# Softplus attention in groups of two stages, and the causal mask added in PSUM by VectorE

## The chip, the cores and the metric

The kernel runs on one core of one Trainium2 chip. The metric is device time in microseconds (us) of one execution. Before the change three runs took 6087.67 us in the median, 6085.19 to 6090.55.

TensorE (PE in the profile) multiplies matrices from SBUF into PSUM, VectorE (DVE), ScalarE (ACT) and GpSimd (POOL) work on elements, and SyncE (SP) issues DMAs. The engines run side by side and wait for each other through semaphores.

## What is computed

Eight layers follow each other on `x` of 8 x 256 x 128 in float32. The change touches two of them, one early and one late:

```python
def _L0_attn_b_ref(X, Wq, bq, Wk, bk, Wv, bv, sink_scalars, v_nulls, Wo, bo):   # softplus attention
    scores = jnp.einsum('bhtd,bhsd->bhts', q, k) * ATTN_SCALE     # 64 heads of 8
    w = jax.nn.softplus(scores / denom)
    w = jnp.where(causal[None, None], w, 0.0)
    w = w * jax.nn.sigmoid(SCALE * w)
    alpha = 1.0 / (jnp.sum(w, axis=-1, keepdims=True) + sinks + 1e-06)
    ...
def _L1_attn_b_ref(x, wq, wk, wv, wo):                            # causal softmax attention
    scores = jnp.einsum('bhqd,bhkd->bhqk', q, k) * scale          # 16 heads of 8
    scores = jnp.where(causal_mask, -jnp.inf, scores)
    local_max = jnp.max(scores, axis=-1, keepdims=True)
    exp_scores = jnp.exp(scores - local_max)
    local_sum = jnp.sum(exp_scores, axis=-1, keepdims=True)
    attn_num = jnp.einsum('bhqk,bhkd->bhqd', exp_scores, v)
    attn_out = attn_num / (local_sum + 1e-08)
```

## The kernel before

The program is eight parts, one after the other; at the end of each all engines meet. Order, tiles and semaphore counts are written out by hand for each engine, so the order in the source is the order on each engine. The parts before, between and behind the two touched ones are the same code before and after.

**Softplus attention (`b0_...`).** One batch entry has 16 units (a unit is one key head with its four query branches), that is 8 pairs and 4 stages of two pairs. Each pair has 3 chunks (keys of block 0 against queries of block 0, then 1 against 1, then 0 against 1), so a stage has 6 chunks and the batch entry 24; eight entries give 32 stages and 192 chunks. A chunk is 128 x 1024 elements and goes this way:

- `scores` (PE, L2220): two float32 matmuls with 32-row keys into two PSUM banks. Chunk kind k always uses banks 2k and 2k+1, so chunk i waits until VectorE is done with chunk i-3 (`b0_soft`).
- `soft` (ACT, L2302 and L2304): exp from PSUM to the buffer `b0_w`, then ln(1+x) in place. Both are in one table set, which `log_exp_tables` (its load is recorded at L312) brings in.
- `larger` (DVE, L2375): the larger of that and the score.
- `weigh` (ACT, L2310): one Silu over all of a pair, 3072 columns; it needs another table set, so a load stands ahead of it.
- `mask` (POOL, L2461): zeroes the upper triangle, one instruction for each unit, two for each pair.
- `heads` (PE, L2234 and L2237): weights times values into PSUM bank 6, then `evacuate` (DVE, L2380), `turn` (PE, four transposes, L2245, bank 7) and `context` (DVE, L2394 to L2408).

`b0_w` holds 8 units, four pairs. So the first chunk of pair p waits in `soft` until `heads` of pair p-4 is done (`b0_out`, L2300). ACT does `soft` of a stage, then `weigh` of that stage. On PE the scores of the next stage stand between the heads of this one (`stage`, L2248 to L2260), and the first three scores of the stage after that stand at its end. Before the first of each six scores PE waits for masked keys (`masked_keys`, DVE L2368), which DVE makes at the end of its stage.

**Causal attention (`b1_...`).** 8 batch entries of 8 units, 64 units; a unit is two heads. Per unit: PE puts the mask into two PSUM banks with an identity matmul (L1922, 256 columns for each of two heads) and adds the scores over it (L1928, three pieces of 128 columns for each head); DVE takes two maxima (`shift`, L2064 and L2065); ACT does four exps with row sums (`exps`, L2020); DVE inverts the sums (`reciprocals`, L2071 and L2073); POOL scales the probabilities (L2097); PE transposes them (`turn`, L1938, six); ACT copies the result to SBUF (`copy_turned`, L2028); PE multiplies with the values (`heads`, L1954). PE runs `scores(u+2)`, `turn(u-1)`, `heads(u-2)` in that order, and `scores(u+2)` waits until `exps(u)` has read the same two banks. Once for each entry PE also projects keys and queries (L1903) and values (L1911) and DVE makes four masked copies of the queries (`mask`, L2059).

A float32 matmul in the source is two instructions in the trace, a transpose is one.

## Time and profile before

| | us |
|---|---|
| median of three runs | 6087.67 |
| profiled execution | 6097.43 |
| its span in the trace | 6095.6 |
| softplus attention, first exp to last Silu, 2747 to 3446 | 699 |
| causal attention, first mask matmul to last heads, 5643 to 5887 | 244 |

| engine | busy us | share of the span |
|---|---|---|
| PE (matmul) | 4834.0 | 79% |
| PE weight load | 3081.1 | 51% |
| ACT | 4289.3 | 70% |
| DVE | 4177.5 | 69% |
| POOL | 2641.0 | 43% |

The shares are averages over parts with different limits, so the two touched parts have to be read by themselves. PEclk in the profile is the TensorE clock that the chip granted, as a share of 2.4 GHz; it is either 1.00 or 0.50 (1.2 GHz), and a figure between is a stretch with both. Over the whole run it is 0.873.

### The profile page before, as it was taken

The page shows a single profiled execution, that of the slowest core. Times are in us where ns is not written, and L with a number is a line of the kernel's source. Part 1 is how long each engine was busy: PE and PEld are TensorE (multiplying, and loading weights), DVE is VectorE, ACT ScalarE, POOL GpSimd, SP SyncE. Part 2 cuts the span into 40 slices and gives each one's busy share as a digit, 9 for nine tenths or more (in the row PEclk, how much of TensorE's full clock was granted, in tenths as well). Part 3 has the DMA queues.
Part 4 walks back from the last instruction along what each step waited for, and adds up shares of the span by engine and source line. Part 5 has one row for each costly group of instructions (what it writes and reads, how often), then busy time and mean ns, then how long its engine had stood idle before and what let it go on. Part 6 is the DMA issues. An engine that isn't in the chain of part 4 may idle for free. (4 is left out here: it accounts for less than half of the span.)

```text
span 6095.6 us, 174670 instructions
## 1 busy us (share of the span) xinstructions
PE 4834.0 (79%) x68176; PEld 3081.1 (51%) x68176; DVE 4177.5 (69%) x6507; ACT 4289.3 (70%) x8575; POOL 2641.0 (43%) x1155
## 2 busy tenths in 40 slices
PE   1000089999999999987777799999999999969998
PEld 0000056666666666642333366666666666624754
DVE  6777767777777777765555477777777777656446
ACT  4444267777777777738999777777777777648668
POOL 0000066555555656513444466565656565400430
PEclk6555589999999999986666699999999999979999
DMA  1000022222222222210000122222222222100000
GB/s 51 0 0 0 29 52 65 61 65 58 62 65 61 65 62 65 54 27 1 0 0 0 31 51 65 62 65 62 64 62 65 62 65 61 48 10 4 1 3 8
DMA packets 181346, 248.41 MB, mean 41 GB/s; under 512 B 52077, under 2 KB 80233, under 8 KB 180073
## 3 DMA queue, kind: packets, MB, share of 16 engines
q1 hardware_dynamic: 176264, 221.95, 14.7%
q10 hardware_dynamic: 4320, 15.73, 0.9%
q8 instruction: 548, 8.98, 0.6%
q14 instruction: 214, 1.75, 0.1%
HBM read 43.50 MB, written 5.24 MB: 8 GB/s over the span
## 5 line engine op out<-in xcount | busy, mean ns | idle before, releaser
L402 PE MATMUL PS<-arena 128*128 128x512 f32 x2304 | 1202.9, 619 | 29.2 <-ACT arena L766 17.7
L1089 POOL TENSOR_TENSOR lns<-arena 128x1024 f32<-128x1024 f32 x192 | 543.8, 2832 | 1009.7 <-DVE arena L975 749.9
L1089 POOL TENSOR_TENSOR arena<-arena 128x1024 f32<-128x1024 f32 x192 | 548.4, 2856 | 468.7 <-DVE arena L975 468.7
L964 DVE TENSOR_REDUCE arena<-arena 128x32 f32<-128x2048 f32 x192 | 438.9, 2286 | 431.3 <-ACT arena L766 431.3
L461 PEld LDWEIGHTS PS<-arena 64*64 64x64 f32 x24576 | 492.9, 136 | 202.2 <-issue 201.4
L1486 PE MATMUL PS<-arena 128*128 128x512 f32 x8 | 5.9, 900 | 700.3 <-DVE arena L1415 700.3
L1092 POOL TENSOR_TENSOR lnc<-arena 128x1024 f32<-128x1024 f32 x192 | 548.5, 2857 | 0.0
L1092 POOL TENSOR_TENSOR arena<-arena 128x1024 f32<-128x1024 f32 x192 | 547.7, 2853 | 0.0
L461 PE MATMUL PS<-arena 64*64 64x32 f32 x24576 | 523.2, 223 | 11.2 <-issue 10.0
L402 PEld LDWEIGHTS PS<-arena 128*128 128x128 f32 x2304 | 378.0, 192 | 253.4 <-issue 113.9
L2461 POOL TENSOR_TENSOR arena<-arena 128x1024 f32<-128x1024 f32 x128 | 298.0, 2357 | 478.3 <-ACT arena L2310 478.3
L765 ACT ACTIVATE arena<-PS 128x512 f32<-128x512 f32 x768 | 471.8, 614 | 32.4 <-PE PS L402 20.9
L766 ACT ACTIVATE arena<-PS 128x512 f32<-128x512 f32 x768 | 476.6, 621 | 0.0
L768 ACT ACTIVATE arena<-PS 128x512 f32<-128x512 f32 x384 | 230.3, 600 | 339.1 <-PE PS L402 338.5
L975 DVE TENSOR_TENSOR arena<-arena 128x1024 f32<-128x1024 f32 x384 | 458.8, 1236 | 8.9 <-ACT arena L781 8.9
L790 ACT ACTIVATE arena<-PS 128x512 f32<-128x512 f32 x768 | 446.4, 620 | 13.7 <-PE PS L419 6.8
L2220 PE MATMUL PS<-arena 32*128 32x512 f32 x768 | 324.7, 968 | 162.7 <-DVE arena L2368 132.7
L959 DVE TENSOR_TENSOR arena<-arena 128x1024 f32<-128x1024 f32 x192 | 429.8, 2239 | 25.5 <-PE PS L422 5.3
L477 PE MATMUL PS<-arena 128*128 128x256 f32 x1536 | 360.1, 386 | 65.6 <-ACT arena L815 65.6
L434 PE MATMUL PS<-arena 64*32 64x64 f32 x24576 | 381.5, 217 | 32.8 <-issue 25.1
L2375 DVE SCALAR_TENSOR_TENSOR arena<-arena,PS 128x1024 f32<-128x1024 f32 x192 | 230.7, 1215 | 242.0 <-ACT arena L2304 241.7
L434 PEld LDWEIGHTS PS<-arena 64*32 64x32 f32 x24576 | 341.8, 105 | 84.6 <-issue 84.4
(278 smaller groups left out, 10919.4 us busy)
## 6 DMA issues: line engine op xcount, KB each, us to landing
arena<-arena SPq DMA_DIRECT2D x2880, 64.0 KB, 2.0
arena<-in_L_ffn_Wqkv ACTq DMA_DIRECT2D x30, 512.0 KB, 4.2
arena<-in_L_ffn_Wo SPq DMA_DIRECT2D x48, 128.0 KB
scratch<-arena SPq DMA_DIRECT2D x4, 1024.0 KB, 4.7
arena<-scratch SPq DMA_DIRECT2D x4, 1024.0 KB, 7.7
arena<-in_L_ffn_W SPq DMA_DIRECT2D x12, 341.0 KB, 2.9
arena<-in_L_ffn_Wqkv SPq DMA_DIRECT2D x6, 512.0 KB, 5.0
arena<-in_ffn_scales SPq DMA_DIRECT2D x12, 128.0 KB, 3.0
```

The lines of the kernel that those rows point to most:

```text
L402: pe.matmul(PS[:, QKV + bank, :], xs[uu % 2][:, par * P:(par + 1) * P], w, start=True, stop=True).then_inc(qkv_ready, 1)
L434: last = pe.matmul(PS[w * WIN:(w + 1) * WIN, SCORE + s, m * FD:(m + 1) * FD], qT[s * FD:(s + 1) * FD, m, w * WIN:(w + 1) * WIN], KT[uu % 2 ...
L461: last = pe.matmul(PS[(m % 2) * FD:(m % 2 + 1) * FD, HEAD + head_index(tt, s) % 2, at:at + WIN], VW[par][rows, w, m * FD:(m + 1) * FD], PT ...
L477: last = pe.matmul(PS[:, HEAD + n % 2, 0:T], Wo[:, m, :], AT[uu][:, m, :], start=(m == 0), stop=(m == PAIRS - 1))
L765: act.activation(chunk(raws[tt % 2], c), PS[:, QKV + bank, :], ACT.Copy)
L766: act.activation(chunk(sq, c), PS[:, QKV + bank, :], ACT.Square).then_inc(qkv_copied, 1)
L790: act.activation(to, PS[:, TURN + n % 2, :].rearrange("p (m t) -> p m t", m=4), ACT.Copy)\
L959: dve.tensor_tensor(EN.rearrange("p (m s e) -> p s m e", s=2, e=FD), E.rearrange("p (s m e) -> p s m e", s=2, e=FD), rc, ALU.mult).then_in ...
L964: dve.tensor_reduce(nrm[:, 3, :], h3(sq), AX_X, ALU.add).then_inc(norm2_own, 1)
L975: dve.tensor_tensor(h3(raw[:, part]), h3(raw[:, part]), rn, ALU.mult).then_inc(u_ready, 1)
L1089: pool.tensor_tensor(halves(heads(t2)), halves(heads(raws[par]))[:, :, ::-1, :], sine, ALU.mult)\
L1092: pool.tensor_tensor(heads(t1), heads(raws[par]), cosine, ALU.mult).then_inc(t1_ready, 1)
```

## The change

**Softplus attention.** Stages are taken two by two. ACT runs `soft` of two stages, 12 chunks, and then `weigh` of both, four Silus; `log_exp_tables` is called before every second `soft` only. `stage` on PE and DVE becomes `group`, of four pairs and 12 chunks, with a new interleaving: 15 scores instead of 9 stand ahead of the loop, and in a group PE runs heads, score 3, turn, heads, scores 4 and 5, turn, heads, scores 6 and 7, turn, score 8, heads, score 9, turn, scores 10 to 14 (numbers count from the next group's first chunk). DVE makes the masked keys of the stages ahead in `keys_ahead`, once behind `larger` 6 and once behind `larger` 11. The buffers are the same.

**Causal attention.** The mask matmul goes. The scores start their banks themselves, in two pieces for each head (128 and 256 columns) where there were three. DVE adds the mask in place in PSUM, 128 x 512 elements over the two banks, waits for its own add, and then takes the two maxima.

```diff
@@ causal attention, PE
-                for s in range(2):
-                    pe.matmul(PS[:, (u % 2) * 2 + s, 0:2 * P], ident[:], b1_mask, start=True, stop=False,
-                              skip_group_check=True)
-                for q, lo, hi in ((0, 0, P), (P, P, 2 * P), (P, 2 * P, BLOCKS)):
+                for q, lo, hi in ((0, 0, P), (P, P, BLOCKS)):
                     for s in range(2):
...
-                                         b1_ks[b % 2][rows, lo:hi], start=(lo == 2 * P), stop=True, skip_group_check=True)
+                                         b1_ks[b % 2][rows, lo:hi], start=True, stop=True)
@@ causal attention, DVE
                 dve.wait_ge(hd_scores, first + u + 1)
+                diagonal = PS[:, (u % 2) * 2:(u % 2) * 2 + 2, 0:2 * P]
+                mask = b1_mask.rearrange("p (o j) -> p o j", o=1).broadcast_to([P, 2, 2 * P])
+                dve.tensor_tensor(diagonal, diagonal, mask, ALU.add).then_inc(b1_added, 1)
+                dve.wait_ge(b1_added, u + 1)
                 dve.tensor_reduce(st[:, 0:2], PS[:, (u % 2) * 2:(u % 2) * 2 + 2, 0:P], AX_X, ALU.max, negate=True)
@@ softplus attention, ACT
             def soft(b, n):
-                log_exp_tables(act)
+                if n % 2 == 0:
+                    log_exp_tables(act)
...
-                for n in range(STAGES):
-                    soft(b, n)
-                    weigh(b, n)
+                for n in range(GROUPS_B0):
+                    soft(b, 2 * n)
+                    soft(b, 2 * n + 1)
+                    weigh(b, 2 * n)
+                    weigh(b, 2 * n + 1)
@@ softplus attention, DVE, in group()
+                evacuate(b, 4 * n + 2)
+                ahead(6)
+                if not final:
+                    keys_ahead(b, 2 * n + 4, 12 * (n + 1) + 5)
+                context(b, 4 * n + 2)
...
+                ahead(9, 10, 11)
+                if not final:
+                    keys_ahead(b, 2 * n + 5, 12 * (n + 1) + 11)
```

The order on PE in softplus attention, from the written-out last two entries. Before, a stage goes on so from the second half of its first pair's heads (L2234 and L2237 are heads, four such rows for each pair, L2220 a score, x2 for each chunk, L2245 a turn):

```order
L2234 MATMUL PS<-arena 32x256 x4
L2237 MATMUL PS<-arena 32x128 x4
L2220 MATMUL PS<-arena 128x512 x2
L2245 MATMUL PS<-ident,arena 128x128 x4
L2220 MATMUL PS<-arena 128x512 x2
L2234 MATMUL PS<-arena 32x256 x4
L2237 MATMUL PS<-arena 32x128 x4
```

With the change a group goes on so from the last heads row of its first pair (L2237 and L2240 are heads, L2223 a score, L2248 a turn):

```order
L2240 MATMUL PS<-arena 32x128 x4
L2223 MATMUL PS<-arena 128x512 x2
L2248 MATMUL PS<-ident,arena 128x128 x4
L2237 MATMUL PS<-arena 32x256 x4
L2240 MATMUL PS<-arena 32x128 x4
L2237 MATMUL PS<-arena 32x256 x4
L2240 MATMUL PS<-arena 32x128 x4
L2223 MATMUL PS<-arena 128x512 x4
L2248 MATMUL PS<-ident,arena 128x128 x4
```

The second pair's heads moved ahead of the second score, and still stand behind the first one.

On ACT, between the last ln of a stage and the first exp of the next, it was before:

```order
L2304 ACTIVATE arena<-arena 128x2x512
L2310 ACT_TABLE_LOAD
L2310 ACTIVATE arena<-arena 128x3072
L2309 REGISTER_ALU
L2310 ACTIVATE arena<-arena 128x3072
L312 ACT_TABLE_LOAD
```

and after 12 chunks it is now (L2314 is the ln, L2320 the Silu):

```order
L2314 ACTIVATE arena<-arena 128x2x512
L2320 ACT_TABLE_LOAD
L2320 ACTIVATE arena<-arena 128x3072 x3
L2319 REGISTER_ALU
L2320 ACTIVATE arena<-arena 128x3072
L312 ACT_TABLE_LOAD
```

The two loads now enclose four Silus in place of two.

On PE in causal attention one unit was before:

```order
L1922 MATMUL PS<-arena,ident 128x256 x2
L1928 MATMUL PS<-arena 128x128 x6
L1938 MATMUL PS<-ident,arena 128x128 x6
L1954 MATMUL PS<-arena 32x256 x2
L1954 MATMUL PS<-arena 32x128 x2
```

and is now (L1926 are the scores, L1936 the transposes, L1952 the heads):

```order
L1926 MATMUL PS<-arena 128x128 x2
L1926 MATMUL PS<-arena 128x256 x2
L1936 MATMUL PS<-ident,arena 128x128 x6
L1952 MATMUL PS<-arena 32x256 x2
L1952 MATMUL PS<-arena 32x128 x2
```

The identity matmuls with full rows and columns are gone, and the score pieces of 128 columns became one of 256.

## Rows read from the trace of the kernel before

**Rows 1.** Busy us by stretch: PE, weight load, DVE, ACT, POOL; PEclk; DMA share, GB/s.
```profile
2747.00:3446.00 699.00, 526.82 (x3001) 216.47 (x3003) 364.01 (x798) 640.50 (x511) 291.26 (x126) 0.62 0.00 1
...
5470.00:5590.00 120.00, 120.00 (x908) 64.00 (x908) 82.66 (x163) 109.48 (x454) 13.97 (x24) 1.00 0.01 1
...
5650.00:5660.00 10.00, 10.00 (x45) 7.49 (x44) 3.82 (x12) 4.36 (x18) 4.22 (x6) 0.50 0.01 2
5661.00:5876.00 215.00, 215.00 (x1823) 151.36 (x1821) 90.53 (x264) 151.54 (x569) 94.24 (x117) 1.00 0.01 1
```
**Rows 2.** Groups by line, 2640 to 3480: shapes xcount | busy us, mean ns | idle before.
```profile
L2304 ACT ACTIVATE arena<-arena 128x1024 f32<-128x1024 f32 x192 | 202.9, 1057 | 6.1
L2302 ACT ACTIVATE arena<-PS 128x1024 f32<-128x1024 f32 x192 | 194.6, 1013 | 51.1 <-PE PS L2220 50.7
...
L2310 ACT ACT_TABLE_LOAD x32 | 41.1, 1283 | 0.6
```
**Rows 3.** Timeline of ACT: start us, us, engine line op [idle before <-releaser].
```profile
3005.26 1.28 ACT L2310 ACT_TABLE_LOAD   x1
3006.55 5.42 ACT L2310 ACTIVATE arena<-arena 128x3072 f32<-128x3072 f32 x2
3011.99 1.28 ACT L312 ACT_TABLE_LOAD   x1
...
3026.23 1.28 ACT L2310 ACT_TABLE_LOAD   x1
...
3049.32 1.28 ACT L2310 ACT_TABLE_LOAD   x1
```
**Rows 4.** Timeline of PE, DVE and POOL in softplus attention.
```profile
3009.46 9.32 POOL L2461 TENSOR_TENSOR arena<-arena 128x1024 f32<-128x1024 f32 x4 [11.60 <-ACT arena L2310]
...
3015.43 1.22 DVE L2375 SCALAR_TENSOR_TENSOR arena<-arena,PS 128x1024 f32<-128x1024 f32 x1 [7.65 <-ACT arena L2304]
...
3022.92 1.13 PE L2220 MATMUL PS<-arena 32*128 32x512 f32 x4
...
3037.76 2.08 PE L2220 MATMUL PS<-arena 32*128 32x512 f32 x4 [0.33 <-DVE arena L2375]
...
3039.77 1.11 PE L2245 MATMUL PS<-ident,arena 128*128 128x128 f32 x4
...
3042.82 1.08 PE L2234 MATMUL PS<-arena 128*32 128x256 f32 x8
...
3044.95 0.66 PE L2237 MATMUL PS<-arena 128*32 128x128 f32 x8
```
**Rows 5.** Timeline of the end of softplus attention: last Silus, last context.
```profile
3440.59 5.42 ACT L2310 ACTIVATE arena<-arena 128x3072 f32<-128x3072 f32 x2
...
3457.35 0.42 DVE L2408 TENSOR_REDUCE XN<-arena 128x16 f32<-128x64 f32 x2
```
**Rows 6.** Timeline of PE over one unit of causal attention, at PEclk 1.00.
```profile
5740.95 1.13 PE L1922 MATMUL PS<-arena,ident 128*128 128x256 f32 x4
...
5742.02 0.94 PE L1928 MATMUL PS<-arena 32*128 32x128 f32 x12
...
5742.88 0.88 PE L1938 MATMUL PS<-ident,arena 128*128 128x128 f32 x6
...
5743.69 0.84 PE L1954 MATMUL PS<-arena 128*32 128x256 f32 x8
```
**Rows 7.** Timeline of PE early in causal attention, where PEclk rises from 0.50.
```profile
5655.92 1.65 PE L1928 MATMUL PS<-arena 32*128 32x128 f32 x12
5657.50 1.54 PE L1938 MATMUL PS<-ident,arena 128*128 128x128 f32 x6
5658.84 1.91 PE L1903 MATMUL PS<-XN,arena 128*128 128x256 f32 x4
5660.54 1.33 PE L1922 MATMUL PS<-arena,ident 128*128 128x256 f32 x4
```
**Rows 8.** Timeline: the nearest DVE operation with an operand in PSUM and 512 columns.
```profile
5889.69 0.69 DVE L2085 TENSOR_TENSOR XO<-XO,PS 128x512 f32<-128x512 f32 x1 [0.17 <-PE PS L1980]
```

More of the change, by code:

```diff
@@ L2103, in program @@
         STAGES = UNITS // 4
+        GROUPS_B0 = STAGES // 2
         BLOCK_KEYS = ((0, 0), (1, 1), (0, 1))
@@ L2246, in turn, with group, ahead @@
                 last.then_inc(b0_turned, 1)
-            def stage(b, par, n, final):
-                def ahead(c):
-                    if not (final and (6 * (n + 1) + c) >= CHUNKS):
-                        scores(b, par, 6 * (n + 1) + c)
-                heads(b, par, 2 * n)
-                ahead(3)
-                turn(b, 2 * n)
-                ahead(4)
-                heads(b, par, 2 * n + 1)
-                ahead(5)
-                turn(b, 2 * n + 1)
-                for c in range(6, 9):
-                    ahead(c)
-            for i in range(9):
+            def group(b, par, n, final):
+                def ahead(*chunks):
+                    for c in chunks:
+                        if not (final and (12 * (n + 1) + c) >= CHUNKS):
+                            scores(b, par, 12 * (n + 1) + c)
+                heads(b, par, 4 * n)
+                ahead(3)
+                turn(b, 4 * n)
+                heads(b, par, 4 * n + 1)
+                ahead(4, 5)
+                turn(b, 4 * n + 1)
+                heads(b, par, 4 * n + 2)
+                ahead(6, 7)
+                turn(b, 4 * n + 2)
+                ahead(8)
+                heads(b, par, 4 * n + 3)
+                ahead(9)
+                turn(b, 4 * n + 3)
+                ahead(10, 11, 12, 13, 14)
+            for i in range(15):
                 scores(0, 0, i)
@@ L2265, in b0_tensor @@
                 for par in range(2):
-                    for n in range(STAGES):
-                        stage(it * 2 + par, par, n, False)
+                    for n in range(GROUPS_B0):
+                        group(it * 2 + par, par, n, False)
             for par in range(2):
-                for n in range(STAGES):
-                    stage(B - 2 + par, par, n, par == 1)
+                for n in range(GROUPS_B0):
+                    group(B - 2 + par, par, n, par == 1)
             pe.wait_ge(b0_done, PAIRS_B0 * B + 1)
@@ L2312, in b0_scalar @@
             with act.Fori(0, B) as b:
-                for n in range(STAGES):
-                    soft(b, n)
-                    weigh(b, n)
+                for n in range(GROUPS_B0):
+                    soft(b, 2 * n)
+                    soft(b, 2 * n + 1)
+                    weigh(b, 2 * n)
+                    weigh(b, 2 * n + 1)
             for c in range(NCH):
@@ L2434, in b0_vector @@
             masked_keys(0, 1)
-            for i in range(6):
+            for i in range(12):
                 larger(0, i)
+                if i == 6:
+                    keys_ahead(0, 2, 5)
+            keys_ahead(0, 3, 11)
             with dve.Fori(0, B // 2 - 1) as it:
                 for par in range(2):
-                    for n in range(STAGES):
-                        stage(it * 2 + par, par, n, False)
+                    for n in range(GROUPS_B0):
+                        group(it * 2 + par, par, n, False)
             for par in range(2):
-                for n in range(STAGES):
-                    stage(B - 2 + par, par, n, None if par == 0 else True)
+                for n in range(GROUPS_B0):
+                    group(B - 2 + par, par, n, None if par == 0 else True)
             for c in range(NCH):
```

27 lines of the change are left out of this document (16 added, 11 removed).

## The prediction

> **What bounds the kernel now.** I read the busy times by stretch first, then the groups by line and the waits, then the timeline of one stage or unit, because the shares of the whole run mix parts with different limits. The two touched parts have different bounds.
>
> In softplus attention ACT is the bound: busy 640.5 of 699 us [rows 1]. Its stage is two table loads, two Silus and six exp and ln. From the first load of the timeline to the end of the second there are 8.01 us (1.28 + 5.42 + 1.28 and small steps), and an exp and an ln take 1.013 + 1.057 us, 2.0 from exp to exp since neighbours overlap [rows 2, 3]. So ACT's own stage is 8.0 + 12.0 = 20.0 us, and 32 of them 641. The other 58 us are nearly all one wait, exp for the scores, 51.1 us [rows 2]. PE is no bound by its work, but its clock is: 0.62 on average [rows 1]. A score takes 2.01 us at half clock and 1.13 at full [rows 4]. Stages are therefore uneven, 20.97 and then 23.09 us between the same loads [rows 3].
>
> In causal attention PE is the bound without a gap: 215.00 of 215 us busy at a clock of 1.00, while ACT has 151.5, DVE 90.5 and POOL 94.2 [rows 1]. There are 59 units in that stretch, 3.64 us each. One unit is 1.07 us of mask matmul, 0.86 of scores, 0.81 of transposes and 0.77 of heads, start to start, 3.51 in all, and 0.13 for the projections [rows 6].
>
> **The change part by part.** The sum is made on the profiled execution, 6097.43 us; the median is 9.8 us lower, and I move only the difference over to it.
>
> *Table loads.* 16 groups need 32 loads where 32 stages needed 64. That is 32 x 1.283 = 41.1 us of ACT, on the path that sets the end [rows 3]. ACT's own group is 2.57 + 4 x 2.71 + 24.1 = 37.5 us, against 40.1 for two stages. The trace shows no other cost of a switch: the Silus start at 3006.55, 1.29 us after the first load, and end at 3011.97, and the next load starts at 3011.99 [rows 3]. The Trainium skill (ScalarE: Activation LUTs, What ACT_TABLE_LOAD costs) gives 1283 ns for the load and about 1380 ns more for a drain with every switch. By it the saving would be 85 us; the load agrees with the trace, the drain is not to be seen beside it, and the sum goes by the row.
>
> *What the wide group gives back.* All eight units of `b0_w` now belong to one group, so the next group's exp for pair p waits for this group's heads of pair p, and on PE those heads stand behind scores which wait for ACT. I walk one group at half clock, with zero at its first Silu. ACT finishes four Silus and a load at 12.2 and the first exp and ln at 14.2. DVE takes 1.22 [rows 4], so score 3 starts at 15.5. POOL's masks are no limit: eight at 2.33 us from 2.9 on [rows 4], the second pair's ready at 12.2. From 15.5 on PE never waits: scores 3 to 11 (9 x 2.01), four turns (4 x 1.05) and three heads (3 x 2.7, from 3042.82 to 3045.61 less the overlap) are 30.4 us [rows 4], so score 11 is there at 45.9. An exp, an ln and a load later the next Silu starts: 49.2 us. Where two scores follow directly each takes about 0.2 less, which gives 48.2. The first wait is the new one: heads of the second pair end at 15.5 + 2.0 + 1.05 + 2.7 = 21.2, and ACT wants that buffer at 18.2. At full clock I estimate a turn at 0.6 and heads at 1.4; the same chain is 15.5 + 10.2 + 2.4 + 4.2 = 32.3, ACT's own work ends later, and only about 1.1 us of waits stay: 38.7.
>
> So a group costs 38.7 to 49.2 us, against 40.1 to 46.2 before, where the mean was 699 / 16 = 43.7, some 6 parts in 10 of the way up. The same place in the new range is about 44.0 to 44.3, and I take 44.0: 16 x 44.0 = 704, **+5 us**. The loads' 41 us are then all given back. At the end 11.8 us passed from the last Silu's end (3446.0) to the last context [rows 5]. Now eight masks (18.6) run from 2.9 us behind the first of four Silus, and heads, copy, turn and context (5 us) come after, 26.5 in all, 15.6 behind the last Silu: **+4 us**. Moved key copies (0.35 us of DVE) lie beside ACT's work, DVE being busy 364 of 699 us [rows 1]; uncovered all 32 would be 11 us. Softplus attention: **+9 us**, bounds -76 (16 x 38.7, with the end) and +92 (16 x 49.2).
>
> *The mask.* PE loses 1.07 us in each of 64 units [rows 6]. The wider score pieces stream the same columns, so I leave the scores at 0.86. DVE gains an add with a PSUM operand, 0.69 us by the nearest row [rows 8]; that row writes to SBUF, and writing back to PSUM could cost more, so 0.6 to 1.0 with the wait on itself, 0.74 taken. DVE's unit goes from 90.5 / 59 = 1.53 to 2.27, below the rest. Behind the add on DVE stand the reciprocals of the unit before, and POOL and then the transposes wait for those; POOL needs 94.2 / 59 = 1.6 us a unit and has room.
>
> **At full clock** PE is then at 3.64 - 1.07 = 2.57 us a unit and ACT at 151.5 / 59 = 2.57 [rows 1]. With two engines equal, four engines in a ring (scores, add and maxima, exps, then scores into the same banks), and four query masks on DVE in one unit of eight, I add 0.2 of waits: 2.77, or (3.64 - 2.77) x 64 = **-56 us**, 2.6 to 2.85 as bounds.
>
> **At half clock** scores are 1.5 us (12 pieces took 1.58), transposes 1.34, a projection 1.70 [rows 7], heads an estimated 1.4 from 0.77 at full [rows 6], the value projection an estimated 0.85. A unit is 4.25 + (1.70 + 0.85) / 8 = 4.6 us, PE again without a gap, 64 are 295 us. Before they took 244, the half-clock start included: **+51 us**.
>
> Which of the two holds decides the sign. Before, PE started this part at half clock and stayed there for a stretch busy 10.00 of 10 us [rows 1], so being busy was not enough. It rose to 1.00 at 5660.5, right behind transposes and a projection of full rows and columns with no gap [rows 7]. The mask matmul was the full-size half of PE's work in the start-up and a third in the steady unit; what is left beside the transposes is 32-row scores and 32-column heads. In softplus attention, where PE has just such scores and heads, the clock kept falling back and gave 0.62 [rows 1]. Against this stands the attention behind: only narrow matmuls, 1.00 for 120 us [rows 1]; but there PE has no gap, while here it would idle some 7%. I hold the fall the likelier, since the new part also has to climb from half clock first, with one projection in eight units to help.
>
> The sum: 6087.7 + 9 + 51 = **6148 us**.
>
> **The rivals.**
> 1. *The clock climbs and holds in causal attention*, decided at the first projection (second batch entry) and kept if PE's idle 0.2 us a unit does not matter. Speaks for it: the 120 us at 1.00 of the part behind. 6087.7 + 9 - 56 = 6041 us, faster.
> 2. *It switches back and forth*: half of the units at each level give 6087.7 + 9 - 2 = 6095, between 6060 and 6120.
> 3. *Softplus attention finds more full clock*, since PE has a long dense stretch in each group: half of the way from 44.0 to 38.7 is -42 us, 6106 with the forecast's causal part. It speaks against it that PE now idles from about 9 to 15.5 in each group, just before its dense stretch.
> 4. *A switch costs more than its load*, a drain that the rows hide under the last ln. By the page's rule named above 44 us more would go: 6104 us. Ends and starts 0.02 us apart [rows 3] leave it little room.
>
> **How the numbers follow.** Forecast 0.52, rival 1 0.28, rival 2 0.13, rival 3 0.05, rival 4 0.02. Faster by over 0.2% means under 6075.5, slower over 6099.9, about what a measurement can tell from no change. Rival 1 is all faster, of rival 2 0.04 faster, 0.05 same and 0.04 slower, of rivals 3 and 4 0.01 same: faster 0.32, same 0.06, slower 0.62. The forecast's own range is 6120 to 6175. The range takes in rival 1 with a unit of up to 2.6 us, 6030, and above the forecast a group of 45: 6164.
>
> **What would show it.** 32 loads for Silu become 16. A wait of exp for heads (L2300's semaphore) at the fourth chunk of a group of about 3 us where PEclk is 0.50. Groups of 44 us. In causal attention PEclk near 0.50, PE still without idle time, scores of 1.5 us, 4.6 us a unit; if PEclk is 1.00 there and units take 2.8 us, rival 1 is right and the step on the clock wrong. An add of over 1.0 us would make DVE the bound.

## The result and the profile after

The changed kernel takes **6017.5 us** (median of 3, 6001.08 to 6021.87) where the kernel before takes 6087.67. The ratio on record is 0.9876, 95% interval 0.9859 to 0.9893; the two medians themselves divide to 0.9885. It is 70 us faster; the prediction said 60 us slower. Its profiled execution has a span of 6015.7 us, 79.9 less than before.

Its page, the busy times and the granted clock in 40 slices:

```profile
span 6015.7 us, 173669 instructions
...
PE 4693.8 (78%) x67664; PEld 2987.3 (50%) x67664; DVE 4249.3 (71%) x6571; ACT 4238.6 (70%) x8543; POOL 2640.4 (44%) x1155
...
PEclk6555599999999999986666699999999999989999
```

PE is 140 us less busy than before, which is more than was gained, and DVE 72 us more. Where the time went is told by the starts of a few instructions in both traces. Five stretches: to the first exp of softplus attention; from there to its last Silu; on to its last context's reduction; the feed-forward part behind it, to its last matmul; and the causal part, from its first score or mask matmul to its last heads. Each is from start to start.

| us | to first exp | to last Silu | to last context | feed-forward | causal part |
|---|---|---|---|---|---|
| before | 2752.2 | 691.1 | 14.2 | 1874.8 | 243.7 |
| after | 2750.8 | 675.4 | 17.8 | 1866.2 | 185.7 |

**Causal attention gained 58.0 us and softplus attention 12.1**: together the 70 us of the medians. The other 9.8 us of the profiled executions are in code that the change does not touch. That code varies from one profiled execution to the next: over all kernels of this study the first stretch takes from 2735.8 to 2754.8 us, and the feed-forward part from 1866.2 to 1874.8 in the twelve kernels without extra matmuls in softplus attention. In the four that have such matmuls it takes 1876.4 to 1893.5, which is hardly chance and comes up again below. So the experiments are read by the two touched stretches first, and then by the whole time.

The changed kernel by stretch: us, busy (x instructions) of PE, PEld, DVE, ACT and POOL, granted clock, DMA share, GB/s. The first is softplus attention up to its last Silu, the third the start of the causal part, the fourth the rest of it to the last heads.

```profile
2750.80:3428.90 678.10, 460.29 (x2960) 183.11 (x2957) 386.38 (x775) 597.06 (x479) 286.10 (x124) 0.66 0.00 0
3428.90:3452.30 23.40, 18.51 (x134) 10.26 (x133) 12.87 (x43) 2.48 (x6) 10.91 (x6) 0.67 0.00 1
5617.00:5632.50 15.50, 10.87 (x50) 7.24 (x50) 10.93 (x24) 7.09 (x31) 3.39 (x5) 0.50 0.00 1
5632.50:5807.00 174.50, 163.65 (x1424) 103.38 (x1422) 132.83 (x330) 154.53 (x593) 100.25 (x124) 1.00 0.01 2
```

Against [rows 1]: softplus attention has a clock of 0.66 where it had 0.62, and the causal part is at 1.00 for all of its steady stretch, with PE idle for 10.9 of 174.5 us. By this row the prediction's own sign says that its step on the clock was wrong: it expected a clock near 0.50 there.

The groups of softplus attention (busy us, mean ns | idle before), to be held against [rows 2]:

```profile
L2314 ACT ACTIVATE arena<-arena 128x1024 f32<-128x1024 f32 x192 | 203.0, 1057 | 6.1
...
L2312 ACT ACTIVATE arena<-PS 128x1024 f32<-128x1024 f32 x192 | 194.3, 1012 | 79.5 <-PE PS L2240 49.6 <-PE PS L2223 28.9
...
L2320 ACT ACT_TABLE_LOAD x16 | 20.5, 1283 | 0.3
```

Of the 32 loads for Silu 16 are gone, and each exp and ln costs what it did. ACT's wait for PE grew from 51.1 to 79.5 us, and 49.6 of that is a wait for the heads (L2240 is their last matmul), where before 50.7 of the 51.1 us were for scores. One group on ACT's timeline shows it:

```profile
2774.94 1.28 ACT L2320 ACT_TABLE_LOAD   x1
2776.24 10.72 ACT L2320 ACTIVATE arena<-arena 128x3072 f32<-128x3072 f32 x4
2786.98 1.28 ACT L312 ACT_TABLE_LOAD   x1
...
2797.70 1.02 ACT L2312 ACTIVATE arena<-PS 128x1024 f32<-128x1024 f32 x1 [3.31 <-PE PS L2240]
...
2807.10 1.03 ACT L2312 ACTIVATE arena<-PS 128x1024 f32<-128x1024 f32 x1 [3.16 <-PE PS L2223]
...
2815.74 1.02 ACT L2312 ACTIVATE arena<-PS 128x1024 f32<-128x1024 f32 x1 [0.52 <-PE PS L2223]
...
2819.87 1.28 ACT L2320 ACT_TABLE_LOAD   x1
```

Four Silus, one load, three exp and ln, then 3.31 us of waiting at the fourth chunk; once more at the seventh, for a score. The 15 intervals from load to load are 44.9 us once and then 41.7 to 43.5. The same group, from its first Silu, up to where the clock rises and on to the next load:

```profile
2776.24:2806.30 30.06, 19.62 (x124) 8.01 (x124) 12.63 (x25) 24.15 (x17) 18.54 (x8) 0.50 0.00 1
2806.30:2819.90 13.60, 10.02 (x72) 4.08 (x68) 10.28 (x26) 12.07 (x13) 0.00 (x0) 1.00 0.00 1
```

In each interval the clock is at 1.00 for 13.6 to 17.1 us, late in PE's dense stretch.

The causal part by operation at full clock, the new add (L2064) and the three lines that it stands between:

```profile
L2018 ACT ACTIVATE arena<-PS,arena 128x128 f32<-128x128 f32 x122 | 48.4, 396 | 11.8 <-DVE arena L2067 11.8
L2064 DVE TENSOR_TENSOR PS<-PS,arena 128x512 f32<-128x512 f32 x60 | 41.7, 695 | 31.0 <-PE PS L1926 31.0
...
L1926 PEld LDWEIGHTS PS<-arena 32*128 32x128 f32 x480 | 31.4, 185 | 22.0 <-ACT arena L2018 9.8 <-issue 7.2 <-DVE arena L2057 4.1
L1926 PE MATMUL PS<-arena 32*128 32x128 f32 x240 | 29.4, 321 | 8.6 <-ACT arena L2018 6.4 <-DVE arena L2057 2.3
```

DVE waits for the scores, the exps for DVE's maxima (L2067), the scores for the exps and for the query masks (L2057). PE's 8.6 us are no wait of every unit: they are one of 0.91 us and one of 0.32 in each of seven batch entries, around the unit in which DVE makes the query masks (L2057). Apart from the end of the part PE has no other gap, so it is still the bound.

### The profile page after: what moved, and what is told of

Same layout as the page of the kernel before. It is cut to its first block and busy times, and to the rows that moved or that the text cites. A ratio compares the mean times of both kernels' runs of the same rounds, so it can differ in the third digit from the quotient of the medians.

```text
span 6015.7 us, 173669 instructions
## 1 busy us (share of the span) xinstructions
PE 4693.8 (78%) x67664; PEld 2987.3 (50%) x67664; DVE 4249.3 (71%) x6571; ACT 4238.6 (70%) x8543; POOL 2640.4 (44%) x1155
## 5 line engine op out<-in xcount | busy, mean ns | idle before, releaser
L461 PE MATMUL PS<-arena 64*64 64x32 f32 x24576 | 524.0, 223 | 10.5 <-issue 9.6
L765 ACT ACTIVATE arena<-PS 128x512 f32<-128x512 f32 x768 | 473.1, 616 | 29.7 <-PE PS L402 18.3
L2223 PE MATMUL PS<-arena 32*128 32x512 f32 x768 | 279.9, 835 | 129.0 <-DVE arena L2387 122.3
```

The costliest lines, as they stand in the source:

```text
L461: last = pe.matmul(PS[(m % 2) * FD:(m % 2 + 1) * FD, HEAD + head_index(tt, s) % 2, at:at + WIN], VW[par][rows, w, m * FD:(m + 1) * FD], PT ...
L765: act.activation(chunk(raws[tt % 2], c), PS[:, QKV + bank, :], ACT.Copy)
```

## The experiments

Stretches as in the table above; "softplus" is from the first exp to the last Silu. A clock is the mean of the whole stretch beside it, and a share of full clock s in the expectations is a mean of (1 + s) / 2. The ratio is to the kernel before on the same chip, where its median was between 6087.5 and 6095.86; medians of different kernels can be from different chips.

| kernel | median us | ratio, 95% interval | softplus us, clock | to last context | causal us, clock |
|---|---|---|---|---|---|
| before | 6087.67 | | 691.1, 0.62 | 14.2 | 243.7, 0.96 |
| after | 6017.5 | 0.9876, 0.9859 to 0.9893 | 675.4, 0.66 | 17.8 | 185.7, 0.97 |
| e1_group | 6077.95 | 0.9981, 0.9969 to 0.9993 | 673.6 | 18.3 | 243.7 |
| e2_mask | 6034.7 | 0.9907, 0.9890 to 0.9924 | 691.0 | 14.2 | 185.7 |
| e3_switch | 6069.16 | 0.9963, 0.9948 to 0.9977 | 726.6, 0.66 | 14.5 | 185.7 |
| e6_nomask | 6004.57 | 0.9858, 0.9841 to 0.9874 | 671.9 | 18.3 | 175.2, 0.97 |
| e5_add2 | 6042.61 | 0.9921, 0.9904 to 0.9937 | 672.0 | 18.3 | 217.8, 0.88 |
| e9_add4 | 6123.46 | 1.0054, 1.0037 to 1.0070 | 673.9 | 17.8 | 290.3, 0.79 |
| e16_gap | 6087.11 | 0.9992, 0.9980 to 1.0004 | 673.5 | 18.4 | 255.6, 0.84 |
| e4_order | 6045.55 | 0.9931, 0.9914 to 0.9949 | 704.4, 0.61 | 17.7 | 185.6 |
| e11_fill | 6037.11 | 0.9907, 0.9889 to 0.9923 | 676.3, 0.77 | 19.6 | 185.6 |
| e17_fill32 | 6032.72 | 0.9905, 0.9886 to 0.9923 | 679.4, 0.68 | 22.4 | 185.7 |
| e12_order_warm | 5993.16 | 0.9842, 0.9820 to 0.9865 | 648.4, 0.65 | 17.2 | 185.3 |
| e13_pace_narrow | 6024.29 | 0.9896, 0.9876 to 0.9916 | 659.0, 0.73 | 21.0 | 185.7 |
| e14_prefill_spread | 6009.86 | 0.9872, 0.9840 to 0.9904 | 651.6 | 17.2 | 176.5 |
| e15_both | 5985.57 | 0.9822, 0.9804 to 0.9839 | 648.3, 0.65 | 17.2 | 176.5, 0.97 |

### One half of the change at a time

e1_group is the kernel before with the part of the change in softplus attention alone, e2_mask with the part in causal attention alone (`b1_added`, the two score pieces, the add in `shift`).

> The kernel before with the softplus grouping alone (16 groups, 16 loads for Silu); the causal part keeps its mask matmul. My theory from the two traces: the part from the first exp to the last context went from 705.6 to 693.5 us, so this kernel is 10 to 16 us faster than before, about 6075. The prediction's step said +9, 6097. If most of the 70 us gained came from here by some effect on later parts, it would be below 6050.

> The kernel before with the causal mask on VectorE alone; softplus attention in stages as before. My theory from the two traces: the causal part took 243.7 us from its first mask matmul to its last heads and 185.7 in the changed kernel, and the clock rises to 1.00 within its first 20 us and holds, so -58 us, about 6030. The prediction's step said half clock and +51, 6139. If the clock of the causal part hung on what the softplus grouping left behind, this one would stay at 0.50 for longer and lie above 6060.

The halves add up: 0.9981 x 0.9907 = 0.9888 beside 0.9876 for both. Each stretch of a half is that of the changed kernel within 2 us, so neither half leans on the other, and both steps of the prediction had the wrong sign: +9 where it is about -12, and +51 where it is -58.

### What a table switch costs

```diff
                 for n in range(GROUPS_B0):
                     soft(b, 2 * n)
                     soft(b, 2 * n + 1)
                     weigh(b, 2 * n)
+                    log_exp_tables(act)
                     weigh(b, 2 * n + 1)
```

> The changed kernel with both function tables loaded once more in each group: exp and ln's table between the second and the third Silu, and Silu's again for the third, so 32 more loads and 16 more pairs of switches, at a point where everything behind waits for ACT. If a switch costs its load of 1.283 us and nothing else: +41 us, 6058 where the changed kernel has 6017. If each switch also drains for 1.4 us, as the prediction's rival 4 had it: +85, 6102. If PE's chain were the only bound of a group and the Silus not on it: under +20.

ACT's timeline in e3_switch:

```profile
3089.52 1.28 ACT L2320 ACT_TABLE_LOAD   x1
3090.81 5.42 ACT L2320 ACTIVATE arena<-arena 128x3072 f32<-128x3072 f32 x2
3096.25 1.28 ACT L312 ACT_TABLE_LOAD   x1
3097.54 1.28 ACT L2320 ACT_TABLE_LOAD   x1
```

Two loads and two Silus, 7.98 us of busy time, are followed by the next load 8.02 us behind the first. A drain of 1.38 us with each switch, as the Trainium skill has it (ScalarE: Activation LUTs, What ACT_TABLE_LOAD costs), has no room there. The stretch grew by 51.2 us: 41.1 of loads, and exp's wait from 79.5 to 88.9 us. What grew there is its wait for scores, 28.9 to 43.8 us, while that for heads fell from 49.6 to 44.9; why is not shown. The whole time grew by 52 us. It lies between the two figures expected, and nearer to the loads alone.

### What the add costs, and what idle time does to the clock

e6_nomask leaves the add out, and with it the causal mask altogether. The other three make it more often; this is e5_add2, e9_add4 has 4 for 2, and e16_gap 9 adds in the last unit of eight and one in the others:

```diff
-                dve.tensor_tensor(diagonal, diagonal, mask, ALU.add).then_inc(b1_added, 1)
-                dve.wait_ge(b1_added, u + 1)
+                for again in range(2):
+                    dve.tensor_tensor(diagonal, diagonal, mask, ALU.add).then_inc(b1_added, 1)
+                    dve.wait_ge(b1_added, 2 * u + again + 1)
```

> The changed kernel without its add: the causal mask is left out altogether (other numbers come out). PE's and ACT's work of a unit is that of the changed kernel, DVE has 64 adds less. If PE and ACT bound the unit (2.57 us each by their work) and the add only costs waits in the ring, the 2.74 us unit falls to 2.57 to 2.65: -6 to -11 us against the changed kernel, about 6008. If the add is wholly hidden: no difference. If the ring through DVE is the bound, up to 0.7 us a unit, -45.

> The changed kernel with the add made twice (the mask is so large that twice masks the same). DVE's unit goes from 2.25 to 2.97 us by its own work, over PE's 2.44 to 2.57, so DVE becomes the bound: a unit of 3.0 to 3.1, +17 to +25 us against the changed kernel, about 6038. If each add lies wholly in the chain from the scores to the exps with nothing beside it: +45. PE then idles a fifth of the time; if its clock falls by that, PE's unit at half clock is 4.6 us by the prediction, +115, 6130.

> The changed kernel with the add made four times. DVE's unit is 2.25 + 3 x 0.72 = 4.4 us, PE busy about 55% of it if its clock stays at 1.00: +105 to +120 us, about 6130, and PEclk tells whether idle time of this size brings the clock down. If it falls to 0.50, PE's 4.6 us a unit and DVE's 4.4 in a ring: +125 to +180. The prediction held that idle time of 7% would do; the trace of the changed kernel has 1.00 with 8%.

> The changed kernel with 64 adds more in the causal part, as e5_add2 has, but in one place for each batch entry: the last unit of eight makes nine adds, the others one. The sum of DVE's extra work is the same 44.5 us. In e5_add2, with the idle time spread over the units, the part took 217.8 us at a mean clock of 0.91. If the clock answers to the total of idle time, this one is alike: 215 to 235 us. If it answers to idle time in one piece, as softplus attention has in its 6.4 us wait, it falls to 0.50 behind each of the eight gaps of some 5 us and a part of the following units runs at half clock: 240 to 280 us, mean clock below 0.85. If a gap of that size is nothing to it, the clock stays at 1.00 and the part takes 225 to 230.

The causal part of e6_nomask from where its clock is 1.00, and then that of e5_add2, e9_add4 and e16_gap (columns as above; the windows of e6_nomask and e9_add4 run 9 and 6 us past the last heads):

```profile
5626.60:5800.00 173.40, 170.08 (x1436) 106.33 (x1433) 100.48 (x278) 156.72 (x592) 98.92 (x122) 1.00 0.01 3
```

```profile
5620.00:5833.00 213.00, 188.23 (x1448) 116.70 (x1448) 179.23 (x407) 165.18 (x615) 103.73 (x128) 0.89 0.01 1
```

```profile
5625.00:5920.00 295.00, 217.27 (x1462) 131.02 (x1459) 272.06 (x544) 165.83 (x620) 103.70 (x128) 0.80 0.00 1
```

```profile
5627.00:5883.00 256.00, 194.58 (x1464) 121.49 (x1464) 185.05 (x412) 163.24 (x621) 103.68 (x128) 0.84 0.00 1
```

Without the add the part takes 175.2 us, and the two gaps around the query masks are gone. So the add, 0.695 us on DVE, costs 10.5 us in 64 units, 0.16 a unit, and hides for the rest. It costs them where it meets the query masks: with the add but the masks spread over two units the part takes 176.5 us (e14_prefill_spread below). A second add costs 32 us: DVE is then busy for 179 of 213 us, and the clock drops in places. Four adds cost 105 us, where 105 to 120 were expected if the clock held. It did not hold, but DVE is busy for nearly all of the part, and PE's slower work mostly lies beside it.

e5_add2 and e16_gap have the same 64 adds more. Spread over all units they cost 32 us, in one piece per batch entry 70. The piece on PE's timeline in e16_gap:

```profile
5718.40 0.84 PE L1952 MATMUL PS<-arena 128*32 128x256 f32 x8
5726.02 1.65 PE L1926 MATMUL PS<-arena 32*128 32x128 f32 x8 [6.78 <-ACT arena L2018]
5727.60 1.54 PE L1936 MATMUL PS<-ident,arena 128*128 128x128 f32 x6
...
5730.40 0.92 PE L1926 MATMUL PS<-arena 32*128 32x128 f32 x8
```

After 6.78 us without work, scores take 1.65 us and transposes 1.54 until 5730.4, where they take 0.92 and 0.88 at full clock; this repeats behind every gap, with a granted clock of 0.53 from 5723.8 to 5730.7 and of 0.99 from there to 5754.6. So a gap of this size brings the clock down, each of eight times, and the last of the three things expected of e16_gap, a clock that stays up through the gap, is out. The Trainium skill (TensorE: Matmul & The Clock Gate, HAM oscillation — how this bites in real kernels) names gaps without PE work as what lets the clock fall; e16_gap agrees.

It is not shown that one piece does more than many small ones. The adds are of the same sum, but not PE's idle time, since in e5_add2 most of DVE's extra work lies beside PE's. From the rise of the clock to the last heads:

| kernel | PE idle, us | share | longest piece | at half clock, us |
|---|---|---|---|---|
| after | 10.8 of 174.8 | 6% | 0.91 | 0 |
| e5_add2 | 23.1 of 200.0 | 12% | 1.65 | 34, in 5 spells |
| e16_gap | 57.7 of 244.7 | 24% | 6.78 | 72, in 8 spells |
| e9_add4 | 68.4 of 269.3 | 25% | 3.11 | 99, in 12 spells |

**Many short waits bring the clock down as well as one long one**: e9_add4, with pieces of 3.11 us at most, has more half clock than e16_gap at nearly the same share of idle time. And of the 38 us by which the part is longer in e16_gap than in e5_add2, 33 are PE's longer idle time itself and only 5 its slower work. The changed kernel's idle time, in pieces of 0.91 us at most, leaves the clock at 1.00. Whether that is for its small sum or its small pieces, no run here tells.

### The order in a softplus group

```diff
                 heads(b, par, 4 * n)
-                ahead(3)
                 turn(b, 4 * n)
                 heads(b, par, 4 * n + 1)
-                ahead(4, 5)
+                ahead(3)
                 turn(b, 4 * n + 1)
+                ahead(4, 5)
                 heads(b, par, 4 * n + 2)
...
-                ahead(0)
                 evacuate(b, 4 * n)
-                ahead(1)
                 context(b, 4 * n)
-                ahead(2)
+                ahead(0)
                 evacuate(b, 4 * n + 1)
-                ahead(3)
+                ahead(1)
                 context(b, 4 * n + 1)
-                ahead(4, 5)
+                ahead(2, 3, 4, 5)
```

> The changed kernel with another order in a softplus group: on PE the first pair's turn and the second pair's heads stand before score 3, and on DVE the first pair's evacuate and context stand before the first larger, in the time in which PE and DVE otherwise wait for ACT's Silus, exp and ln. Theory A, the prediction's walk of a group: the 3.3 us wait of exp at the fourth chunk goes, and PE's chain behind score 3 is shorter by a turn and a pair's heads (4.8 us at half clock), so a group falls from 42.7 us to 39 to 41, the kernel by 25 to 55 us, to 5960 to 5995. Theory B: what PE gains in order it loses in clock, since its dense stretch is shorter: the granted clock in the part falls below 0.66 and the time stays within 10 us of the changed kernel.

It came out 28 us slower than the changed kernel, with groups of 43.6 to 48.3 us and a clock of 0.61. The clock fell as Theory B has it, but the time is outside its 10 us, and PE's timeline shows another fault:

```profile
3141.97 2.08 PE L2223 MATMUL PS<-arena 32*128 32x512 f32 x4 [1.67 <-DVE arena L2387]
3143.98 1.11 PE L2248 MATMUL PS<-ident,arena 128*128 128x128 f32 x4
3145.02 2.08 PE L2223 MATMUL PS<-arena 32*128 32x512 f32 x4
3149.97 2.07 PE L2223 MATMUL PS<-arena 32*128 32x512 f32 x4 [2.87 <-DVE arena L2387]
```

Score 5 waits 2.87 us for `larger` 2, which frees its banks and which DVE had behind a context, which itself waited for a turn on PE. e12_order_warm puts `ahead(1, 2)` before that context. It also has a second edit, in the causal part, two matmuls that compute nothing of use behind the second unit's scores:

```diff
             scores(0)
             scores(1)
+            for again in range(2):
+                pe.matmul(PS[:, 4, :], hd_w[0], XN[:, 0:CH], start=True, stop=True)
```

> The changed kernel with two edits in parts that lie apart, each read from its own stretch. Softplus attention: the order of e4_order, with its third larger ahead of the second pair's context on DVE (in e4_order score 5 waited 2.9 us behind that). If that was the fault, its groups fall from 44.5 to 41 or less; if the clock is, the full-clock share stays near 0.22 and groups near 44. Causal part: two matmuls of 128 rows by 512 columns more behind the scores of the second unit, where PE waits 3.6 us at half clock; their product is used by nobody. If the climb to 1.00 hangs on PE's work at the start, it comes sooner than 15.5 us behind the first projection (5632.5 in the changed kernel), and the part falls from 185.7 to 178 to 184 us; if not, it stays within 1 us or grows by up to 2.

Groups fall to 40.0 to 42.3 us, most of them 40.9, the stretch to 648.4 us, and exp's wait to 53.5 us:

```profile
2751.90:3403.00 651.10, 484.18 (x2959) 192.72 (x2957) 385.03 (x775) 596.10 (x479) 287.26 (x124) 0.65 0.00 1
```

The clock is no higher than in the changed kernel, and all of exp's wait is now for scores. So **Theory A holds once DVE's order is right**: the order without the wait at the fourth chunk is worth 27 us, and e4_order's low clock of 0.61 went up to 0.65 with its own wait gone.

### Filler for PE, wide and narrow

e11_fill, in softplus attention, and behind it the one line in which e17_fill32 differs:

```diff
+            def fill(b, p, count):
+                pe.wait_ge(b0_done, nth(b, PAIRS_B0, p) + 1)
+                for again in range(count):
+                    pe.matmul(PS[:, 7, :], ident[:], b0_K[:, 0:CH], start=True, stop=True)
...
+                fill(b, 4 * n - 1, 2)
                 heads(b, par, 4 * n)
+                fill(b, 4 * n - 1, 5)
```

```diff
-                    pe.matmul(PS[:, 7, :], ident[:], b0_K[:, 0:CH], start=True, stop=True)
+                    pe.matmul(PS[:, 7, :], ident[0:32, :], b0_K[0:32, 0:CH], start=True, stop=True)
```

> The changed kernel with 7 matmuls of 128 rows by 512 columns more in each softplus group, in time in which PE otherwise waits (two before the first pair's heads, where it waits 2.9 us for POOL, five behind them, where it waits 6.4 us for DVE); their product goes into a bank that the next turn overwrites. They compute nothing that is used. Theory A: a group's length hangs on the share of full clock in it, and the clock follows how much PE did just before. Then it rises sooner and a group goes from 42.7 towards the 38.7 us that the prediction worked out for full clock: -25 to -60 us against the changed kernel, 5960 to 5990, granted clock in the part over 0.75. Theory B: the clock does not follow filler, or falls again in the dense part: the fillers end beside the waits at half clock too (2.4 and 6.0 us), within 10 us of the changed kernel. Theory C: they end late and push score 3: +10 to +20.

> e11_fill with its seven fillers in a softplus group read from 32 rows in place of 128, of the same 512 columns and so of the same duration by the rows of the causal part (270 ns for 128 columns at either height). With 128 rows the share of full clock in softplus attention went from 0.33 to 0.54. The prediction took the causal part to stay at half clock because its scores and heads are narrow while the mask matmul was not. If narrow matmuls do not lift the clock, the share stays near 0.33 to 0.40 here and the stretch up to the last Silu is over 685 us. If what counts is that PE is busy, the share is 0.50 to 0.58 and the stretch 670 to 680, as in e11_fill.

The softplus stretch of e11_fill, then of e17_fill32:

```profile
2753.60:3433.00 679.40, 564.48 (x3173) 222.39 (x3171) 377.95 (x775) 597.70 (x479) 287.60 (x124) 0.77 0.00 1
```

```profile
2747.40:3430.00 682.60, 605.31 (x3173) 245.83 (x3172) 384.77 (x775) 596.61 (x479) 286.78 (x124) 0.68 0.00 1
```

And the fillers of each by line:

```profile
L2254 PE MATMUL PS<-arena,ident 128*128 128x512 f32 x224 | 131.6, 736 | 3.5 <-issue 3.5
```

```profile
L2254 PE MATMUL PS<-arena,ident 32*128 32x512 f32 x224 | 185.6, 996 | 3.9 <-issue 3.9
```

With 128 rows the clock goes from 0.66 to 0.77. With 32 rows it goes to 0.68, although PE is busier. The two differ in nothing but the rows that the fillers read, so being busy does not lift the clock by itself. **The prediction's view of 32-row matmuls stands here.** That any full-size matmul lifts it does not follow: in the kernel before, identity matmuls of 128 x 128 were nearly half of PE's work at the start of the causal part, and PE was busy without a gap at 0.50 for 17.9 us:

```profile
5643.20:5661.10 17.90, 17.90 (x76) 13.23 (x77) 4.84 (x14) 7.50 (x34) 4.83 (x6) 0.50 0.01 1
```

Yet the higher clock of e11_fill shortens nothing, 676.3 us beside 675.4. It is won in the fillers: from score 3 to the next load, where PE's order counts, the 15 intervals have 223 us at 1.00 in all, beside 219 in the changed kernel. e13_pace_narrow holds the fillers back to end just before score 3:

```diff
+                pe.wait_ge(b0_done, nth(b, PAIRS_B0, 4 * n - 1) + 1)
+                fill(b, 1)
                 heads(b, par, 4 * n)
+                fill(b, 2)
+                pe.wait_ge(b0_weight, nth(b, PAIRS_B0, 4 * n + 3))
+                fill(b, 1)
+                if not (final and n + 1 == GROUPS_B0):
+                    pe.wait_ge(b0_e, nth(b, CHUNKS, 12 * (n + 1)))
+                    fill(b, 1)
```

In the causal part it has four matmuls of 32 rows where e12_order_warm has two of 128.

> The changed kernel with two edits in parts that lie apart, each read from its own stretch. Softplus attention: five matmuls of 128 rows by 512 columns more a group, held back by waits so that they end just before score 3: one ahead of the first pair's heads, two behind them, one behind the last Silu and one behind the first exp. Theory A: with the clock up just ahead of the stretch that counts, a group falls from 42.7 to 40 to 41.5 (-20 to -40 us in all). Theory B, by e11_fill (share of full clock 0.54, but groups no shorter): the clock that is won lies in the fillers, and a group stays at 42 to 43.5. Causal part: four matmuls of 32 rows by 512 columns in the place where e12_order_warm has two of 128 rows. The prediction held that such narrow matmuls do not lift the clock: then it climbs as in the changed kernel (185.7 us). If what counts is that PE is busy, it climbs sooner, as with the wide ones (178 to 184).

The stretch to the last Silu gets 16.4 us shorter, most groups 41.2 us, with 240 us at 1.00 from score 3 on, and the end 3.2 longer. So full clock in the right place shortens the stretch, though less than the order does.

**The whole time does not show it**: 6024.29 us is 7 more than the changed kernel. All kernels with fillers in softplus attention lose time behind it. Their feed-forward part takes 1876.9 us (e11_fill), 1876.4 (e17_fill32), 1879.4 (e13_pace_narrow) and 1893.5 (e14_prefill_spread below), and in no other kernel more than 1874.8. The medians agree for the wide ones: less the three stretches of the table 5155.6, 5158.6 and 5164.6 us are left, 5145.2 for e17_fill32 and 5134.5 to 5143.8 for the twelve others. Nothing is edited there, and why the fillers cost time behind them stays open.

The start of the causal part, in e12_order_warm and in e13_pace_narrow, from the first score to where the clock is 1.00 for good:

```profile
5605.40:5616.80 11.40, 10.15 (x51) 5.75 (x51) 7.62 (x19) 7.07 (x32) 4.20 (x6) 0.66 0.00 1
```

```profile
5625.40:5636.60 11.20, 10.96 (x50) 6.52 (x50) 7.54 (x18) 6.19 (x28) 3.37 (x5) 0.50 0.00 1
```

The same answer as from e17_fill32, in the place that was disputed: the narrow filler keeps PE busy for 10.96 of 11.2 us and the clock at 0.50, the wide one brings a spell of full clock. It falls back, and the part is no shorter for it (185.3 us beside 185.7). In both the clock is at 1.00 for good from some 11 us behind the first score, as in the changed kernel.

### Two more edits, and the best version

e14_prefill_spread is the order of e12_order_warm with one filler ahead of a group's first heads, and makes the query masks of the causal part in two units:

```diff
-                if n == 5 and b + 1 < B:
-                    mask(b + 1)
+                if n in (4, 5) and b + 1 < B:
+                    mask(b + 1, (2 * n - 8, 2 * n - 7))
```

> The changed kernel with two edits in parts that lie apart, each read from its own stretch. Softplus attention: the order of e12_order_warm with one matmul of 128 rows by 512 columns more ahead of the first pair's heads, where PE waits 3.2 us. If the clock is what keeps that order slow, its groups get shorter than those of e12_order_warm by 0.5 to 2 us; if not, equal. Causal part: the four query masks of a batch entry, which DVE makes in one go, are split over two units. PE waited 4.6 us for them in the changed kernel and ACT waited for the maxima behind them: 185.7 us fall to 178 to 183; no change if the ring (scores, add, maxima, exps) is the bound in every unit.

The filler gains nothing (651.6 us beside 648.4). Spreading the masks takes the causal part from 185.7 to 176.5 us, nearly the 175.2 that it has without any add: the add had cost time almost only where DVE also made all four masks. The whole time shows little of either gain, 6009.86 us, since this is the kernel that loses most behind its filler. e15_both leaves the fillers out and keeps the order and the spread masks:

> The changed kernel with the two edits that paid, without any filler: the softplus order of e12_order_warm, and the query masks of the causal part split over two units as in e14_prefill_spread. By their stretches, -27 us in softplus attention (groups of 40.9 us) and -9 us in the causal part (176.5 us): 36 us below the changed kernel, about 5982. If either edit only moved time to a later part, it is above 6000.

5985.57 us, ratio 0.9822 (0.9804 to 0.9839): 110 us faster than the kernel before on the same chip (6095.86), and by the medians 32 faster than the changed kernel. It is the best version of this study.

## Why the prediction was wrong, point by point

**The table loads: right.** 16 loads for Silu in place of 32, 41.1 us with those that go back, and e3_switch shows that a switch costs its load. The drain of rival 4 is not there.

**What the wide group gives back: right in kind, mis-sized.** The new wait stands where it was put, at the fourth chunk, 3.31 us for about 3.0; the end grew by 3.6 us for 4. But the mean group was taken at 44.0 us, "the same place in the new range", and it is 42.4 (678.1 / 16), which is 26 us less in all. The base was off too: the 699 us begin 5.2 before the first exp, and from there to the end of the last Silu it is 693.8, 43.4 a group. Set against that, the +5 is -15.7, and with the end the step's +9 is -12. (Six parts in ten of the new range are also 44.4 us or more and not 44.0; the low base and this slip work against each other.) The clock did not keep its place: 0.66 where it had been 0.62, rival 3's direction, to which I gave 0.05. That the higher clock is what made the groups shorter is argued from the trace; no run holds the order and changes only the clock there. Of the loads' 41.1 us, 28.4 came back as longer waits of exp, and the rest did not.

**The add: right.** 0.695 us for 0.74. e6_nomask prices its cost in the ring at 0.16 us a unit, beside the 0.2 that was allowed. The allowance lumped three reasons together, and only one of them, the query masks, turned out to cost anything much, so that the size fits is in part luck.

**The causal part at full clock: right in size, given too small a chance.** Rival 1 had -56 us, the trace and e2_mask have -58.0. It also named the moment, the first projection of the second batch entry. PE's timeline there reads like [rows 7] without the mask matmuls:

```profile
5629.81 1.54 PE L1936 MATMUL PS<-ident,arena 128*128 128x128 f32 x6
5631.14 1.70 PE L1904 MATMUL PS<-XN,arena 128*128 128x256 f32 x4
5632.77 0.92 PE L1926 MATMUL PS<-arena 32*128 32x128 f32 x8
```

Transposes and projection at half clock, then scores in 0.92 us. The clock rose 11.2 us behind the first score (5621.3 to 5632.5); before, it rose 17.9 us behind the first mask matmul.

**The step that failed** is "I hold the fall the likelier, since the new part also has to climb from half clock first", with its idle 7% a unit. It joined two claims. That narrow matmuls do not lift the clock is what both 32-row fillers show (e17_fill32, and e13_pace_narrow in the disputed place). But the step took the mask matmul to be what had lifted it, and the kernel before speaks against that: its clock stayed at 0.50 through 17.9 us that were nearly half mask matmuls. Both kernels rise right behind the transposes and the projection of the second batch entry, and these were still there. The other claim, that 7% of idle time would bring the clock down again, is false for the 6% that it came to: the clock stands at 1.00 through all of it. With e5_add2's 12% it drops in places.

The step also misread [rows 1]. The 120 us at 1.00 in the attention behind are not "only narrow matmuls":

```profile
L1689 PE MATMUL PS<-XN,arena 128*128 128x256 f32 x24 | 6.8, 405 | 0.0
L1697 PE MATMUL PS<-arena,XN 128*128 128x128 f32 x24 | 4.3, 300 | 0.0
```

These are projections, 11.1 of the 120 us. The causal part without its mask matmuls has more than that: transposes and projections of 128 x 128 are 67.6 of its 174.5 us. So the row does not show that 32-row and 32-column matmuls alone hold the clock, but it still spoke for a clock that holds here, and the chance of 0.52 for half clock had no row behind it. With full clock in the causal part the same sum would have been 6041 us; with the mis-sized group put right as well, 6020.

Still open: what of PE's idle time brings the clock down, its sum or the length of its pieces, and which full-size operations lift it, the transposes, the projection or both. No kernel here took one of them away alone.

## What to carry to other kernels

Ask two questions of TensorE's clock, and answer each from its own rows: what lifts it (here not 32-row matmuls, however busy they keep PE), and what lets it fall (here each gap of 6.8 us, and short waits where they were many, but not the few of the changed kernel). Before taking an operation for the one that lifts the clock, look at how long it ran at half clock. When a widened group makes a new wait on a shared buffer, look for work that can go into the time in which the engine waits for another anyway, and move both engines' orders together: the same move was worth -27 us with DVE's order right and +29 with one operation behind the wrong wait. And where untouched code varies by 10 to 20 us between executions, read an edit from the stretch that it touches, but compare the rest of the time over all kernels as well: the fillers' gain in their stretch was lost behind it.

## What the runs showed of the hardware

A small multiply on DVE with both inputs in SBUF, part of each context, takes 0.29 us, and in the changed kernel up to 2.24. By line before, and then after, it is the same instruction:

```profile
L2404 DVE TENSOR_TENSOR arena<-arena 128x128 f32<-128x128 f32 x64 | 18.9, 296 | 2.2
```

```profile
L2416 DVE TENSOR_TENSOR arena<-arena 128x128 f32<-128x128 f32 x64 | 48.4, 756 | 2.2
```

One of the long ones on the timeline of the changed kernel, and what POOL did then:

```profile
3096.67 2.20 DVE L2416 TENSOR_TENSOR arena<-arena 128x128 f32<-128x128 f32 x1
```

```profile
3080.18 18.55 POOL L2489 TENSOR_TENSOR arena<-arena 128x1024 f32<-128x1024 f32 x8 [24.91 <-ACT arena L2320]
```

POOL's last mask ends at 3098.73 and the multiply at 3098.87. While its neighbours on DVE with an operand in PSUM run on beside POOL's masks at their usual 0.24 and 0.34 us, this one waits for the mask to end. The Trainium skill (SBUF — State Buffer, SBUF: two separate sides) says that a DVE operation with two SBUF inputs and a GpSimd operation that reads SBUF exclude each other for a whole instruction; the trace agrees. Before, the longest of these multiplies took 0.55 us: POOL's four masks were mostly over when a stage's contexts ran, and the eight of a group are not. It costs DVE 29.5 us in all; what it costs the kernel no run here shows.
